# Layer 0 routed experts with 71 tiles in place of 72, and a loop over tiles with a longer written-out end

## The chip, the cores and the metric

One Trainium2 chip, one of its cores. The metric is the device time of one launch of the whole kernel in microseconds (us); all inputs and outputs are in the device's memory. A core has five instruction streams that run side by side and wait for each other by semaphores: PE (TensorE; the profile shows its weight loads apart as PEld), DVE (VectorE), ACT (ScalarE), POOL (GpSimd) and SP (SyncE, here used to issue DMAs). Each stream is a program of its own, with its own loops and branches, and its instructions are brought from memory by DMA too: the profile has them as packets of a kind "instruction", one queue for each engine (q8 is PE's, q14 is DVE's).

## What is computed

A two-layer network on x, 16 batches x 256 tokens x 512 channels (4096 tokens). Cut to what matters:

```python
def reference(x, ctx, g_xattn, g_ffn, ...):
    x = x + tanh(g_xattn[0]) * wkv(w, u, layernorm(x), ctx)              # decaying running average over the tokens
    x = x + tanh(g_ffn[0])   * moe0(layernorm(x))                        # 8 experts, each token uses 2; one shared
    x = x + tanh(g_xattn[1]) * chunked_causal_attention(layernorm(x), ctx, ctx)   # 16 heads of 32, 256 tokens
    x = x + tanh(g_ffn[1])   * moe1(layernorm(x))                        # 64 experts, each token uses 6, room for 64

def moe0(xf):                                                            # 4096 x 512
    ew, ei = top_k(xf @ gate_w.T, 2)
    ew = softmax(ew)
    routed = sum over the 2 chosen e of  ew * ((silu(xf @ w_gate[e].T) * (xf @ w_up[e].T)) @ w_down[e].T)
    return routed + sigmoid(xf @ se_gate_w.T) * shared(xf)
```

The change concerns `routed` of moe0, which the kernel calls its phase `routed0`.

## The kernel before

The kernel runs through four phases, one after the other, with a barrier of all engines between them (L164): `wkv_phase` (layer 0's attention part and the routing and shared expert of moe0, 16 batches), `routed0_phase` (the 8 experts of moe0), `attention_phase` (layer 1's attention, routing and shared expert, 16 batches) and `routed1_phase` (the 64 experts of moe1, in 32 pairs).

**The tiles of routed0.** 4096 tokens choose 2 experts each, which gives 8192 pairs of a token and an expert. They lie in a list in memory, sorted by expert, and each expert's part is worked on in tiles of 128 pairs, the last of an expert with dummies in its open places. 8192 / 128 = 64 tiles would do if each expert's count were a multiple of 128. Each expert may leave one tile part filled, and the kernel runs `TILES0 = N * K0 // P + E0 = 72` of them (L24). An expert's last tile lacks at most 127 pairs, so that (8192 + 8 x 127) / 128 = 71.9 bounds the number of tiles that hold a pair: no routing fills more than 71. The tile past those that the routing fills has all 128 places on a dummy row: it is gathered, run through the matmuls like any other, and its results go to a place out of bounds, which the write leaves out. `tiles_table` works out for each of the 72 tiles its expert and its start in the list, in arrays of 128 x 72 and 128 x 72 x 8.

**One tile.** SP loads the tile's 128 pairs (L2191), POOL gathers the 128 token rows (L2194), PE transposes them (L1047, four blocks; the helper L332 is one matmul of a product of numbers split in a high and a low part), ACT and DVE copy the transposed rows as high part (L1107) and low part (L1161), PE does gate and up (12 matmuls at L332), ACT the silu (L1124), DVE its product with up (L1149), PE transposes h (L1070), ACT and DVE split it (L1112, L1155, L1156), PE does down (L1079 twice as the profile counts, and three at L332), DVE scales by the pair's weight (L1175) and POOL writes the rows out (L1019). The code of one turn of PE holds the transposes of the next tile, gate and up of this one and down of the one before, so that tiles overlap. The turns differ by the tile's place in a ring of `WAYS0 = 8`, since buffers and semaphores are chosen by it (`pair_0` to `pair_7`, `ys_0` to `ys_3`).

**The loop over tiles.** Every engine runs `turns(eng, TILES0, turn, WAYS0)` (L107). It writes out the first `ways + 1` turns, then makes a loop of `count // ways - 2` iterations whose body has `ways` turns, and then writes out the turns that are left. For 72 tiles by eights these are 9 turns (tiles 0 to 8), 7 iterations of 8 (tiles 9 to 64) and 7 turns (tiles 65 to 71). A loop of 7 iterations branches back 6 times. The same helper makes the loops of the two batch phases (16 batches by twos: 3 turns, 6 iterations of 2, 1 turn, so 5 branches back) and of PE in routed1.

**The code behind it.** On each engine the instructions stand in the order of the phases: the loop of `attention_phase` comes after all turns of routed0 that are written out. In the compiled program of DVE an instruction takes 64 bytes. Counted there, the attention loop's first instruction, to which it branches back, is number 1023 of DVE's stream, and its last is number 1373. That is 351 instructions. For PE the loop's first instruction is number 5272, for ACT 667.

Of the kernel before, what the change touches and what calls it, by code (L numbers as in the profile page):

```python
# [14 lines left out]
P = 128  # L15
B, T, C = 16, 256, 512
N = B * T
# [3 lines left out]
DUMMY = P  # L21
E0, H0, S0, K0 = 8, 256, 512, 2
E1, H1, S1, K1, CAP = 64, 352, 704, 6, 64
TILES0 = N * K0 // P + E0  # L24
UNUSED = 2 * K0 * N
LIST0 = E0 * N + P
HEADS, D = 16, 32
# [8 lines left out]
WAYS0, SLOTS0, AHEAD0, READY0 = 8, 4, 3, 2  # L36
# [20 lines left out]
class Chain:  # L57
# [5 lines left out]
    def turn(self, i):  # L63
        assert self.n in (0, self.per), (self.n, self.per)
        self.n, self.base = 0, i * self.per
# [35 lines left out]


def last(count, ways=2):
    return Turn(count - 1, count // ways - 1, ways - 1, count, ways)


def turns(eng, count, turn, ways=2):  # L107


    assert count % ways == 0  # L110
    for n in range(ways + 1):
        turn(Turn(n, n // ways, n % ways, count, ways))
    with eng.Fori(1, count // ways - 1) as j:
        for n in range(1, ways + 1):
            turn(Turn(ways * j + n, j + n // ways, n % ways, count, ways))
    for n in range(count - ways + 1, count):
        turn(Turn(n, n // ways, n % ways, count, ways))


# [13 lines left out]


FIRST, LAST = first(B), last(B)


# [40 lines left out]
class Setup:  # L178
# [35 lines left out]
    def pool(self, nc, pool):  # L214
# [14 lines left out]
                       allow_small_or_imprecise_dtypes=True).then_inc(made, 1)  # L229
        nc.gpsimd.iota(c.tile_no[:], [[1, TILES0]], base=0, channel_multiplier=0,  # L230
                       allow_small_or_imprecise_dtypes=True).then_inc(made, 1)
# [104 lines left out]
def wkv_phase(nc, io, c):  # L336
# [6 lines left out]
    with Memory(nc, "wkv_") as m:  # L343
# [6 lines left out]
        count_i = m.sb("count_i", [P, E0], I32)  # L350
        past = m.sb("past", [P, TILES0, E0])
        past_nt = m.sb("past_nt", [P, TILES0, E0])
        expert, start, row = (m.sb(n, [P, TILES0]) for n in ("expert", "start", "row"))
        table, expert_i, row_i = c.early.table, c.early.expert_i, c.early.row_i
# [55 lines left out]
        with nc.Block() as block:  # L410
# [319 lines left out]
            def _(dve):  # L730
# [119 lines left out]
                def tiles_table():  # L850
# [7 lines left out]

                    every = [P, TILES0, E0]

# [87 lines left out]
def routed0_phase(nc, io, c):  # L948


    with Memory(nc, "routed0_") as m:
# [28 lines left out]
        placed = [m.sem(f"rows_placed{s}") for s in range(SLOTS0)]  # L980
        with nc.Block() as block:
# [5 lines left out]
            def _(sp):  # L987
# [10 lines left out]

                turns(sp, TILES0, turn, WAYS0)

            @block.gpsimd
            def _(pool):
# [33 lines left out]
                turns(pool, TILES0, turn, WAYS0)  # L1036
                place(last(TILES0, WAYS0))
                for s in range(SLOTS0):
                    pool.wait_ge(placed[s], 16 * (TILES0 // SLOTS0))

            @block.tensor
            def _(pe):
# [1293 lines left out]
```

## Time and profile before

| | us |
|---|---|
| three runs | 2252.53, 2248.7, 2243.45 (median 2248.7) |
| the profiled execution, its own time | 2247.8 |
| its span, first to last instruction | 2246.1 |
| routed0's tiles, first silu to the last result's write | 546 to 912 |
| attention, first instruction after the barrier | 917.5 |
| attention's loop on DVE (6 iterations) | 1099.6 to 1743.7 |
| routed1 | 1850 to 2246 |

The span of 2246.1 us lies within 1.7 us of that execution's own time. So a us that is lost or won inside is a us of the time. An engine's share of the span (PE 87%, DVE 58%, POOL 39%, ACT 34%) is a mean over the four phases; the 40 slices of section 2 of the page, 56 us each, show them apart. A row of the timeline is: start, duration, engine, line, operation, output and inputs; in brackets the idle time of the engine ahead of it and what ended it, where "issue" means that no wait in the profile explains it. A row of busy time by stretch is: start and end, length, then for PE, PEld, DVE, ACT and POOL the busy us and in brackets the number of instructions, then the granted TensorE clock (1.00 is 2.4 GHz), the busy share of the DMA engines and the GB/s moved. A row of packets is: queue and kind, packets, MB, the packets' share of 16 engines in that stretch. A row of a line's instructions is: line, engine, operation, count, shortest/median/longest in ns, and the start of the first and the last.

### The profile page before, as it was taken

The numbers are of one execution on the slowest core, as the hardware profiler recorded it, in microseconds if no ns is written. First come the engines' busy times: TensorE is split into PE (matmuls) and PEld (weight loads), VectorE is DVE, ScalarE is ACT, GpSimd is POOL, SyncE is SP. The second block draws the span as 40 slices with busy tenths as digits, with TensorE's granted clock in tenths as the row PEclk, the third lists the DMA queues.
The fourth block names the chain that finished last, engine by engine and source line by source line (L and its number), as shares of the span: only waits on it lengthen the run. The fifth ranks groups of instructions, "written<-read, shape, count | busy, mean of one in ns | idle before, by whom it ended". The sixth has DMA issues, their size and how long they took to land. (4 is left out here: it accounts for less than half of the span.)

```text
span 2246.1 us, 38784 instructions
## 1 busy us (share of the span) xinstructions
PE 1964.9 (87%) x11898; PEld 1394.6 (62%) x11899; DVE 1299.3 (58%) x3013; ACT 757.8 (34%) x2192; POOL 864.8 (39%) x840
## 2 busy tenths in 40 slices
PE   3898888988999999469999999999999969989886
PEld 2666666665777777347777777777777754433332
DVE  6888888885644444237776767776766632222221
ACT  3323333324322222255554545554545411111111
POOL 5556655544543333142333333333333241121221
PEclk9999999999999999669999999999999989989998
DMA  8323222223333332331111121111111249999995
GB/s 257 130 85 94 75 85 83 84 92 101 104 102 102 102 103 95 131 99 67 67 67 68 67 68 67 68 67 68 67 67 67 99 183 416 403 405 404 404 406 173
DMA packets 113560, 319.47 MB, mean 142 GB/s; under 512 B 31298, under 2 KB 39490, under 8 KB 105220
## 3 DMA queue, kind: packets, MB, share of 16 engines
q1 hardware_dynamic: 86388, 264.83, 31.4%
q0 software_dynamic: 26880, 52.68, 8.2%
q8 instruction: 88, 1.44, 0.3%
q14 instruction: 60, 0.49, 0.1%
q10 hardware_dynamic: 144, 0.03, 0.0%
HBM read 257.33 MB, written 62.33 MB: 142 GB/s over the span
## 5 line engine op out<-in xcount | busy, mean ns | idle before, releaser
L1585 ACT ACTIVATE attn_pr<-attn_score_ps,attn_nmax 128x128 f32<-128x128 f32 x496 | 201.5, 418 | 201.2 <-DVE attn_nmax L1733 201.2
L1696 POOL DMA_INDIRECT list<-attn_pair,attn_pos x192 | 191.0, 995 | 65.2 <-issue 61.3
L332 PE MATMUL attn_ffn_ps<-attn_xnT_high,attn_wgu_high 128*128 128x256 f32 x704 | 208.2, 296 | 8.2 <-DVE attn_hT_low L1825 7.3
L332 PE MATMUL attn_ffn_ps<-attn_xnT_low,attn_wgu_high 128*128 128x256 f32 x704 | 199.8, 284 | 0.0
L332 PE MATMUL attn_ffn_ps<-attn_xnT_high,attn_wgu_low 128*128 128x256 f32 x704 | 199.6, 283 | 0.0
L304 POOL TENSOR_SCALAR attn_norm_var_eps<-attn_norm_mean_var 128x2 f32<-128x2 f32 x32 | 7.9, 247 | 474.5 <-DVE attn_norm_mean_var L298 474.5
L532 PE MATMUL wkv_ffn_ps<-wkv_xnT,wkv_wg 128*128 128x256 f32 x512 | 147.3, 439 | 25.1 <-DVE wkv_x L847 24.0
L1981 POOL DMA_INDIRECT out<-routed_ym,routed_place x32 | 50.2, 1568 | 294.7 <-DMA out<-routed_ym,routed_place 274.5
L1733 DVE TENSOR_REDUCE attn_nmax<-attn_score_ps 128x2 f32<-128x256 f32 x248 | 126.3, 551 | 62.9 <-PE attn_score_ps L1422 61.9
L332 PEld LDWEIGHTS attn_ffn_ps<-attn_xnT_high,attn_wgu_high 128*128 128x128 f32 x704 | 135.3, 192 | 18.3 <-DVE attn_hT_low L1825 12.1
L1019 POOL DMA_INDIRECT y<-routed_ys,first_ffn_pair x72 | 73.3, 1017 | 186.1 <-DVE routed_ys L1175 176.3
L532 PEld LDWEIGHTS wkv_ffn_ps<-wkv_xnT,wkv_wg 128*128 128x128 f32 x512 | 107.9, 219 | 50.7 <-DVE wkv_x L847 31.4
L332 PEld LDWEIGHTS attn_ffn_ps<-attn_xnT_low,attn_wgu_high 128*128 128x128 f32 x704 | 135.6, 193 | 0.0
L332 PEld LDWEIGHTS attn_ffn_ps<-attn_xnT_high,attn_wgu_low 128*128 128x128 f32 x704 | 135.3, 192 | 0.0
L1432 PE MATMUL attn_tr_ps<-ident,attn_pr 128*128 128x128 f32 x768 | 115.1, 288 | 21.5 <-ACT attn_pr L1585 21.3
L532 PE MATMUL wkv_ffn_ps<-wkv_xnT,wkv_wu 128*128 128x256 f32 x512 | 122.8, 383 | 0.0
L332 PE MATMUL routed_gu_ps<-routed_wgu_high,routed_xT_high 128*128 x288 | 120.3, 418 | 2.0 <-POOL first_ffn_wgu_low L976 1.8
L1738 DVE COPY second_ffn_room<-attn_tr_ps 128x384 f32<-128x384 f32 x96 | 52.9, 551 | 118.0 <-PE attn_tr_ps L1432 93.3
L1419 PE MATMUL attn_score_ps<-second_ffn_room 32*128 32x256 f32 x992 | 118.7, 358 | 0.7 <-issue 0.7
L332 PE MATMUL routed_gu_ps<-first_ffn_wgu_low,routed_xT_high 128*128 x288 | 113.8, 395 | 0.0
L332 PE MATMUL routed_gu_ps<-routed_wgu_high,routed_xT_low 128*128 x288 | 113.2, 393 | 0.0
L1432 PEld LDWEIGHTS attn_tr_ps<-ident,attn_pr 128*128 128x128 f32 x768 | 87.0, 145 | 41.2 <-issue 32.9
(286 smaller groups left out, 4790.0 us busy)
## 6 DMA issues: line engine op xcount, KB each, us to landing
second_ffn_room<-in_w_gu SPq DMA_DIRECT2D x16, 2816.0 KB, 31.2
routed_wgu<-in_w_gu SPq DMA_DIRECT2D x16, 2816.0 KB, 31.4
second_ffn_room<-in_w_down SPq DMA_DIRECT2D x16, 1536.0 KB, 24.5
routed_wdn<-in_w_down SPq DMA_DIRECT2D x16, 1536.0 KB, 26.1
wkv_x<-in_x SPq DMA_DIRECT2D x32, 512.0 KB, 3.8
second_ffn_room<-y SPq DMA_DIRECT2D x32, 512.0 KB, 5.6
wkv_vT<-in_ctxT SPq DMA_DIRECT2D x16, 512.0 KB, 4.3
xn<-wkv_xn SPq DMA_DIRECT2D x16, 512.0 KB, 2.8
```

Of the source, the lines that this page charges most:

```text
L304: nc.gpsimd.tensor_scalar(self.var[:], self.mv[:, :, 1], EPS, None, ALU.add).then_inc(self.rstd_s, 1)
L332: ins = nc.tensor.matmul(out, a[i], b[j], start=start and n == 0, stop=stop and n == 2)
L532: ins = nc.tensor.matmul(ffn_ps[n % 2][:, col:col + T], w[:, k, n * P:(n + 1) * P], xnT[:, k, :], start=(k == 0), stop=(k == KC - 1))
L1019: nc.gpsimd.indirect_dma_start(io["y0"], bass.IndirectOffsetOnAxis(ap=pair[t.s][:, 1:2].bitcast(U32), axis=0), ys[t.s % SLOTS0][:], None, ...
L1419: nc.tensor.matmul(score_ps[:, a, KEYS[j]], qT[b.s][r:r + D, k, j * P:(j + 1) * P], kT[b.s][r:r + D, k, 0:(j + 1) * P], start=(j == 1), st ...
L1432: ins = nc.tensor.transpose(tr_ps[bank][:, col * P:(col + 1) * P], pr[u % 2][:, z // 3, z % 3, :], c.ident[:])
L1585: nc.scalar.activation(pr[u % 2][:, a, j:2 * j + 1, :].rearrange("p k t -> p (k t)"), score_ps[:, a, KEYS[j]], ACT.Exp, bias=nmax[u % 2][: ...
L1696: nc.gpsimd.indirect_dma_start(io["list1"], bass.IndirectOffsetOnAxis(ap=pos[b.s][:, j, k:k + 1], axis=0), pair[b.s][:, j, k, :], None, bo ...
L1733: v.tensor_reduce(nmax[u % 2][:, :, j], score_ps[:, :, KEYS[j]], AX.X, ALU.max, negate=True).then_inc(max_s, 1)
L1738: v.tensor_copy(prT[u % 4][:, 0].rearrange("p k t -> p (k t)"), tr_ps[0][:, 0:3 * P]).then_inc(tr_ev[0], 1)
L1981: nc.gpsimd.indirect_dma_start(io["out"], bass.IndirectOffsetOnAxis(ap=place[q.s % SLOTS1][:].bitcast(U32), axis=0), ym[q.s % SLOTS1][:], ...
```

## The change

`TILES0` is 71. `turns` no longer asks for a multiple of `ways`: the loop still has `count // ways - 2` iterations, and the written-out end begins after the last of them, wherever that is. For 71 tiles by eights: 9 turns (0 to 8), 6 iterations (9 to 56) and 14 turns (57 to 70), so the loop branches back 5 times. For 16 by twos and 32 by eights the turns are the same ones as before. `last()` gives the place of a last tile that needn't end a round, and POOL's last wait takes the number of writes that each of the four `ys` buffers has had.

```diff
-TILES0 = N * K0 // P + E0
+TILES0 = N * K0 // P + E0 - 1
...
 def last(count, ways=2):
-    return Turn(count - 1, count // ways - 1, ways - 1, count, ways)
+    return Turn(count - 1, (count - 1) // ways, (count - 1) % ways, count, ways)
...
-    assert count % ways == 0
     for n in range(ways + 1):
         turn(Turn(n, n // ways, n % ways, count, ways))
     with eng.Fori(1, count // ways - 1) as j:
         for n in range(1, ways + 1):
             turn(Turn(ways * j + n, j + n // ways, n % ways, count, ways))
-    for n in range(count - ways + 1, count):
+    for n in range((count // ways - 1) * ways + 1, count):
         turn(Turn(n, n // ways, n % ways, count, ways))
...
                 for s in range(SLOTS0):
-                    pool.wait_ge(placed[s], 16 * (TILES0 // SLOTS0))
+                    pool.wait_ge(placed[s], 16 * -(-(TILES0 - s) // SLOTS0))
```

One line goes from the file, so every line number behind `turns` is one less after the change.

On each engine the seven turns that are added to the written-out end push what comes behind. The listing of DVE's instructions around the start of attention's loop, before; the branch and the ISA at the helper's line open the loop, and what follows is its first turn:

```order
L298 BN_AGGR attn_norm_mean_var<-attn_norm_stats 128x2 x2
L113 UNCONDITIONAL_BRANCH
L113 ISA
L1738 COPY second_ffn_room<-attn_tr_ps 128x384
L1730 ISA
L1733 TENSOR_REDUCE attn_nmax<-attn_score_ps 128x2 x2
L1828 ISA
L1829 SCALAR_TENSOR_TENSOR attn_x_1<-attn_ffn_ps,gate_half,attn_x_1 128x512
```

And after:

```order
L297 BN_AGGR attn_norm_mean_var<-attn_norm_stats 128x2 x2
L112 UNCONDITIONAL_BRANCH
L112 ISA
L1737 COPY second_ffn_room<-attn_tr_ps 128x384
L1729 ISA
L1732 TENSOR_REDUCE attn_nmax<-attn_score_ps 128x2 x2
L1827 ISA
L1828 SCALAR_TENSOR_TENSOR attn_x_1<-attn_ffn_ps,gate_half,attn_x_1 128x512
```

The instructions are the same and in the same order. What moved is their place in the stream: the loop's branch is row 676 of DVE's listing before and row 711 after. The listing puts some instructions in one row and leaves waits out. In the compiled program the loop's first instruction goes from number 1023 to 1086, 63 further. Its last goes from 1373 to 1436. On PE the loop's first goes from 5272 to 5741, and on ACT from 667 to 709. The loops of `wkv_phase` and of routed0 itself stay where they are.

The end of routed0 on DVE, before, with the buffers' numbers in the names (`ys_2` is the third of four buffers for results):

```order
L1149 TENSOR_TENSOR routed0_h<-routed0_silu_gate,routed0_gu_ps1 128x256
L1175 TENSOR_SCALAR routed0_ys_2<-routed0_y_ps0,first_ffn_pair_6 128x512
L1155 TENSOR_TENSOR routed0_hT_low<-routed0_ht_ps,routed0_hT_high 128x128
L1156 COPY routed0_hT_whole<-routed0_ht_ps 128x128
L1175 TENSOR_SCALAR routed0_ys_3<-routed0_y_ps1,first_ffn_pair_7 128x512
L981 UNCONDITIONAL_BRANCH
```

And after:

```order
L1148 TENSOR_TENSOR routed0_h<-routed0_silu_gate,routed0_gu_ps0 128x256
L1174 TENSOR_SCALAR routed0_ys_1<-routed0_y_ps1,first_ffn_pair_5 128x512
L1154 TENSOR_TENSOR routed0_hT_low<-routed0_ht_ps,routed0_hT_high 128x128
L1155 COPY routed0_hT_whole<-routed0_ht_ps 128x128
L1174 TENSOR_SCALAR routed0_ys_2<-routed0_y_ps0,first_ffn_pair_6 128x512
L980 UNCONDITIONAL_BRANCH
```

The phase ends with the same instructions, one place earlier in the ring: the last tile is 70 in place of 71, and uses `ys_2` in place of `ys_3`.

## Rows read from the trace of the kernel before

**Rows 1.** The page: the span in 40 slices of 56 us, in tenths.

```profile
PE   3898888988999999469999999999999969989886
DVE  6888888885644444237776767776766632222221
PEclk9999999999999999669999999999999989989998
DMA  8323222223333332331111121111111249999995
```

**Rows 2.** Busy time by stretch (columns as in the section on the profile).

```profile
588.60:869.90 281.30, 280.35 (x1289) 212.70 (x1288) 126.44 (x280) 63.72 (x169) 111.67 (x113) 1.00 0.32 101
869.90:903.90 34.00, 34.00 (x157) 25.92 (x156) 15.12 (x34) 7.42 (x20) 11.43 (x12) 1.00 0.25 81
917.00:1000.00 83.00, 43.27 (x256) 29.96 (x256) 26.45 (x57) 39.43 (x116) 29.78 (x25) 0.58 0.43 144
```

**Rows 3.** Timeline of PE in routed0: the down product of two neighbouring tiles.

```profile
869.65 1.02 PE L1079 MATMUL routed_y_ps<-first_ffn_down,routed_hT_whole 128*128 x2
874.64 1.02 PE L1079 MATMUL routed_y_ps<-first_ffn_down,routed_hT_whole 128*128 x2
```

**Rows 4.** The silu of each tile: duration min/median/max in ns, first and last start.

```profile
L1124 ACT ACTIVATE routed_silu_gate<-routed_gu_ps x72: 383/383/384, 546.1 to 904.3; 128x256 f32<-128x256 f32 x72
```

**Rows 5.** Timeline of PEld: the first transpose after one of routed0's branches back.

```profile
630.16 0.42 PEld L1047 LDWEIGHTS routed_xt_ps<-ident,first_ffn_xg 128*128 128x128 f32 x4 [0.61 <-issue]
```

**Rows 6.** Waits from 590 to 903: us in total, times, longest us.

```profile
POOL y L1019 <- DVE routed_ys L1175: 168.3, 61, 4.0
ACT routed_silu_gate L1124 <- PE routed_gu_ps L332: 138.3, 62, 2.2
DVE routed_ys L1175 <- PE routed_y_ps L332: 46.7, 63, 0.8
```

**Rows 7.** Timeline from the last tile to the first instruction of attention.

```profile
909.10 0.75 DVE L1175 TENSOR_SCALAR routed_ys<-routed_y_ps,first_ffn_pair 128x512 f32<-128x512 f32 x1 [2.10 <-PE routed_y_ps L332]
910.69 0.98 POOL L1019 DMA_INDIRECT y<-routed_ys,first_ffn_pair  x1 [2.27 <-DVE routed_ys L1175]
917.54 0.20 DVE L1871 TENSOR_SCALAR attn_limit<-base 128x64 f32<-128x64 f32 x1 [7.70 <-PEq L164]
```

**Rows 8.** The loop's branch: DVE in attention, DVE in routed0, ACT in attention.

```profile
L113 DVEq COMPARE_BRANCH  x1: 63/63/63, 1313.8 to 1313.8; - x1
L113 DVEq FUSED_REGOPS  x1: 85/85/85, 1318.4 to 1318.4; - x1
L113 DVEq COMPARE_BRANCH  x1: 74/74/74, 630.1 to 630.1; - x1
L113 DVEq FUSED_REGOPS  x1: 70/70/70, 630.3 to 630.3; - x1
L113 ACTq COMPARE_BRANCH  x1: 45/45/45, 1308.0 to 1308.0; - x1
L113 ACTq FUSED_REGOPS  x1: 78/78/78, 1308.2 to 1308.2; - x1
```

**Rows 9.** Timeline of DVE: first instruction behind each of attention's five branches.

```profile
1210.05 0.56 DVE L1738 COPY second_ffn_room<-attn_tr_ps 128x384 f32<-128x384 f32 x1 [5.00 <-issue]
1318.53 0.56 DVE L1738 COPY second_ffn_room<-attn_tr_ps 128x384 f32<-128x384 f32 x1 [4.61 <-issue]
1425.21 0.56 DVE L1738 COPY second_ffn_room<-attn_tr_ps 128x384 f32<-128x384 f32 x1 [4.77 <-issue]
1532.16 0.56 DVE L1738 COPY second_ffn_room<-attn_tr_ps 128x384 f32<-128x384 f32 x1 [5.32 <-issue]
1640.31 0.56 DVE L1738 COPY second_ffn_room<-attn_tr_ps 128x384 f32<-128x384 f32 x1 [4.91 <-issue]
```

**Rows 10.** Timeline: what DVE does behind that branch, and the PE that waits.

```profile
1319.01 1.01 DVE L1733 TENSOR_REDUCE attn_nmax<-attn_score_ps 128x2 f32<-128x256 f32 x2
1319.93 0.74 DVE L1829 SCALAR_TENSOR_TENSOR attn_x<-attn_ffn_ps,gate_half,attn_x 128x512 f32<-128x512 f32 x1
1320.73 0.66 PE L1401 MATMUL attn_ffn_ps<-ident,attn_xn 128*128 128x128 f32 x4 [1.11 <-DVE attn_x L1829]
```

**Rows 11.** Instruction packets by queue: whole kernel, 1250:1357, 1315:1318, 1320:1323.

```profile
q8 instruction: 88, 1.44, 0.3%
q14 instruction: 60, 0.49, 0.1%
q8 instruction: 9, 0.15, 0.5%
q14 instruction: 5, 0.04, 0.1%
q14 instruction: 1, 0.01, 1.4%
q14 instruction: 1, 0.01, 0.7%
```

**Rows 12.** Timeline of PEld behind the loop's branch near 1205.

```profile
1206.88 0.19 PEld L332 LDWEIGHTS attn_ffn_ps<-attn_wd_high,attn_hT_high 128*128 128x128 f32 x1
1208.75 0.19 PEld L332 LDWEIGHTS attn_ffn_ps<-attn_wd_low,attn_hT_high 128*128 128x128 f32 x1 [1.69 <-issue]
```

**Rows 13.** Timeline of PEld: the same transposes in three batches in a row.

```profile
1251.72 0.64 PEld L1432 LDWEIGHTS attn_tr_ps<-ident,attn_pr 128*128 128x128 f32 x6 [1.49 <-issue]
1304.19 0.64 PEld L1432 LDWEIGHTS attn_tr_ps<-ident,attn_pr 128*128 128x128 f32 x6 [1.49 <-issue]
1359.77 0.64 PEld L1432 LDWEIGHTS attn_tr_ps<-ident,attn_pr 128*128 128x128 f32 x6 [1.49 <-issue]
```

## The prediction

> **What bounds the kernel now.** I read the page's 40 slices first, since the phases have different limits, and the change touches one phase and moves the code of the ones behind it [rows 1]. routed0 is slices 10 to 16: PE is at 9 there and DVE at 4. In its steady part PE is busy 280.35 of 281.30 us, and 34.00 of 34.00 in its last stretch, at a clock of 1.00 [rows 2]. The table of waits agrees: ACT, POOL and DVE all wait for what PE or the one behind PE makes, and PE has no row of that size [rows 6]. So routed0 costs what PE's matmuls cost. Attention is slices 19 to 31: PE is at 9 again, but I looked there for the branches of its loop, because that code is moved. Its first 83 us run at a mean clock of 0.58, whatever stands ahead of them in routed0 [rows 2]. routed1 is bound by DMA (9 in its slices) and is left as it is.
>
> **The tile that goes.** Two tiles in a row stand 874.64 - 869.65 = 4.99 us apart [rows 3]. The silu confirms 72 tiles between 546.1 and 904.3, a mean of 5.05 with the slower first ones [rows 4]. PE runs without a gap in the last stretch, so nothing hides the tile: -4.99. The tile that goes is a late one, with no work on the expert's weights. Its gather, list load and write on POOL and SP go too. They lie under PE. The end of the phase, from the last tile's scaling at 909.10 to attention's first instruction at 917.54, has the same steps on one tile earlier [rows 7], and costs what it did. The arrays of the tile table shrink from 72 to 71 columns, which is 1/72 of a few DVE operations, under 0.1 us.
>
> **The branch that goes.** The loop branches back 5 times in place of 6. Behind a branch PE's weight load has a gap of 0.61 us which no wait explains [rows 5]. Against the steady period of 4.99, the six tiles behind a branch come 0.38, 0.40, 0.36, 0.39, 0.33 and 0.12 us late. One of them goes: -0.33, between -0.12 and -0.40. Sum of the direct parts: -5.3.
>
> **The longer written-out end.** 14 turns in place of 7 are read once, in a row. PE has about 67 instructions in a turn, so a packet of 16 KB (below) lasts some four tiles, 19 us, and fetching one took under 5 us wherever I could see it. The written-out end of before shows no stop in PE: busy 34.00 of 34.00 [rows 2]. Cost 0. If that cover were gone, each of two more packets would cost 2 to 5 us. DVE, ACT and POOL have 9, 6 and 8 instructions in a turn, and wait half of the time [rows 6].
>
> **The moved code: where the sum is decided.** Attention's loop branches back 5 times, on every engine. Behind DVE's branch at 1313.8 the next instruction starts at 1318.4. The same branch in DVE's routed0 loop takes 630.1 to 630.3, and ACT's in attention 1308.0 to 1308.2 [rows 8]. All five of DVE's stand 4.61 to 5.32 us with nothing waited for [rows 9]. What fills that time is a fetch of instructions: an iteration has 5 packets of 0.04 MB on q14, 8 KB or 128 instructions each, one of them between branch and resumption, and the next about 3 us after the resumption, in 1320 to 1323 [rows 11]. In 640 to 860, inside routed0's loop, no queue has an instruction packet. The same transposes of PE stand 1304.19 - 1251.72 = 52.47 us apart without a branch and 1359.77 - 1304.19 = 55.58 with one [rows 13]. Over the five branches the surplus is 1.5 to 3.6 us, 12.5 in all: half of DVE's stop comes through to PE.
>
> Why does DVE's loop fetch and ACT's doesn't? DVE's has 351 instructions. ACT's has 262, three blocks of 128. I take it that DVE holds four blocks, one of which is the one being fetched ahead. A loop that touches four has thrown out its first by the time it branches back. Where the blocks begin comes from PE: after a branch back it stops for 1.69 us, at 1208.75, in the middle of a product in which nothing is waited for [rows 12], and again for 1.13 at 1638.51. Counted in the program that is the 42nd instruction of the loop, number 5314. So PE's blocks of 256 (16 KB packets on q8) have 62 instructions ahead of the stream's first. If DVE has the same 62 (the times of its packets in straight code allow 61 to 67), its loop starts at (1023 + 62) mod 128 = 61 of a block before, and 67 instructions of that block follow: enough to run while the next block comes. **After the change it starts at (1086 + 62) mod 128 = 124.** Four instructions are left: set the registers, the copy at L1738, a register, and one of the two reductions at L1733. The block with the rest isn't there. It was usable about 4.9 us after resumption before, since the next packet came 2.9 to 3.3 us behind the resumption and an instruction runs some 1.9 us behind its packet. So the second reduction, which began 0.9 us after the resumption [rows 10], begins 4.9 after it: 4.0 us later. PE already waits 1.11 us for the L1829 that follows it [rows 10], so nothing is left to hide it. I take 3.8 of the 4.0, since PE's own stop of 1.69 goes (its loop start gets 85 instructions of rest in place of 42). Bounds: 3 (part absorbed as with the first stop) to 5 (a whole second stop, as in rows 9); the floor is 0, if the next block is fetched together with the first. Five branches: 5 x 3.8 = +19.0, from +15 to +25.
>
> The loop still touches four blocks (124 + 351 = 475, under 512), so its first stop stays. ACT's loop goes from offset 89 to 3 of a block and touches three both times. POOL's and SP's stay small.
>
> **Sum**, against the profiled execution's own 2247.8 (the median of the runs is 0.9 above it): 2247.8 - 5.0 - 0.3 + 19.0 = **2261.5**, for this case 2256 to 2268.
>
> A rule of the Trainium skill stands against this. Its page "Runtime: NRT & Kernel Launch", section "Instruction fetch mechanics", has an engine's instruction memory refilled in blocks of 16 KiB, prefetched in order, says that a taken branch whose target isn't in the window forces a fetch before execution goes on, and therefore favours unrolling. The trace agrees on the fetch behind a taken branch, but DVE's packets are 8 KB here. With 256-instruction blocks the loop would have a long rest either way, and the sum would be rival A's.
>
> **Rivals.**
> A: *the place of the code doesn't matter.* Either the next block is asked for together with the first, or my 62 is wrong by enough to leave a long rest. Then only the direct parts count: 2247.8 - 5.3 = **2242.5**. For it: I have not seen DVE stop for want of a second block, and the 62 is carried over from PE. Against it: PE did stop so, in two of five branches, when its second packet came 4.4 us behind the first. 0.19.
> B: *the loop's start falls on or just behind a block's start.* That takes 66 or 67 ahead in place of 62. Then the loop touches three blocks, as ACT's does, it stays in the buffer, and DVE's five stops go with the 12.5 us that they cost: 2247.8 - 5.3 - 12.5 = **2230**. For it: four instructions decide, and packet times allow it. Against it: PE's stop gives 62 exactly. 0.11.
> C: *a second stop at each branch*, the forecast and the case on the slower side. It decides if between 1 and 6 instructions of rest are left behind the branch, and is slower as soon as a stop costs over 5.3 / 5 = 1.1 us: **2261.5**. 0.70.
> That the change doesn't do what it says is no case of its own: the tile is in the program whatever its rows hold (72 silus [rows 4]), so dropping it drops its work. Attention's slow clock at its start hangs on PE's idle time at the barrier, which stays.
>
> **How the numbers follow.** The predicted time is C's. The range reaches from A's 2242.5, less 1.5 for the branch's and the runs' spread, to C's upper end: 2241 to 2268. It leaves out B and the ends of C. The three runs lie within 0.25% of their median, so that 0.5% (11.2 us) is about what can be told from no change. B is faster by more. A is within. C is slower by over 0.5% where its sum is above 2259.5, about two thirds of its chance: slower 0.47, and same 0.19 + 0.23 = 0.42.
>
> **What would show each step.** The window of routed0's tiles shorter by 5.3 us, silu x71, PE gapless up to the last tile. DVE's first instruction behind each of attention's five branches still 4.6 to 5.3 us late, and then a second gap with "issue" as its reason ahead of the second L1732 or the first L1828, 3 to 5 us: C. No such gap, the first ones as they were: A. None of both and fewer q14 packets in an iteration: B. The period of the transposes with a branch would be 58 to 60 us in C, about 55 in A and 52.5 in B. PE's stop of 1.69 should be gone in all. The forecast is wrong if DVE's blocks aren't where I counted them, or if the fetch of the second block starts before the first is used.

## The result, and the profile after

The change makes the kernel slower. In the median the kernel before takes 2251.8 us (8 runs) and the changed one 2269.5 us (8 runs, 2263.9 to 2279.7). The ratio is 1.008 with a 95% interval of 1.0061 to 1.0099. The prediction said slower, by +13.7 us, and gave 2241 to 2268. The direction and the place were right. The size was too small, and the median lies 1.5 us above the range.

The profiled execution took 2268.25 us with a span of 2266.5, against 2246.1 before. It divides at three instructions that both traces have: the last silu of a tile, and DVE's first and sixth branch at the end of attention's loop.

| stretch | before | after | difference |
|---|---|---|---|
| start to the first silu | 546.1 | 544.1 | -2.0 |
| first to last silu (72 or 71 tiles) | 358.2 | 353.0 | -5.2 |
| last silu to DVE's first branch | 300.7 | 303.1 | +2.4 |
| five iterations, first branch to sixth | 538.7 | 562.2 | **+23.5** |
| sixth branch to the end | 502.4 | 504.1 | +1.7 |
| sum | 2246.1 | 2266.5 | +20.4 |

The tiles, from the silu's row of after, whose columns are those of [rows 4]:

```profile
L1123 ACT ACTIVATE routed_silu_gate<-routed_gu_ps x71: 383/383/384, 544.1 to 897.1; 128x256 f32<-128x256 f32 x71
```

The branch of attention's loop on DVE, of after (count, shortest/median/longest in ns, first and last start):

```profile
L112 DVEq COMPARE_BRANCH  x6: 55/63/63, 1200.2 to 1762.4; - x6
```

And of before:

```profile
L113 DVEq COMPARE_BRANCH  x6: 55/63/63, 1205.0 to 1743.7; - x6
```

The tiles gave 5.2 us, as the sum had it. The first, third and last stretch vary by themselves: over all kernels below, the first silu stands between 544.1 and 551.8, and the third stretch is 299.6 to 303.4 long (b72_others apart, of which more below). a71_dve2 and a71_dve4, two instructions apart, stand at 299.6 and 303.2. The kernels with 72 tiles have 300.4 to 301.9 and those with 71, but for a71_dve2, 302.1 to 303.4, so that some of the +2.4 may belong to the change; no run separates it. What stands out is the loop.

DVE behind its branches back, timeline of after. [rows 9] have one stop for each branch, here are two:

```profile
1205.61 0.56 DVE L1737 COPY second_ffn_room<-attn_tr_ps 128x384 f32<-128x384 f32 x1 [5.30 <-issue]
1210.35 1.02 DVE L1732 TENSOR_REDUCE attn_nmax<-attn_score_ps 128x2 f32<-128x256 f32 x2 [4.18 <-issue]
...
1317.95 0.56 DVE L1737 COPY second_ffn_room<-attn_tr_ps 128x384 f32<-128x384 f32 x1 [5.57 <-issue]
1322.83 1.02 DVE L1732 TENSOR_REDUCE attn_nmax<-attn_score_ps 128x2 f32<-128x256 f32 x2 [4.32 <-issue]
...
1435.13 1.02 DVE L1732 TENSOR_REDUCE attn_nmax<-attn_score_ps 128x2 f32<-128x256 f32 x2 [4.85 <-issue]
```

The second stop is there at all five branches, 4.18, 4.32, 4.85, 4.25 and 4.30 us. It stands ahead of *both* reductions, so that fewer instructions ran between the stops than the four that the prediction counted. The register instruction ahead of the reductions tells how many. It comes at the end of the second stop, in a row of that line:

```profile
L1729 DVEq FUSED_REGOPS  x1: 46/46/46, 1210.3 to 1210.3; - x1
```

Only the first register instruction and the copy ran before. With two instructions of rest, 64 instructions lie ahead of DVE's stream, not 62.

Who waits for it is PE, on PE's timeline of after. At the same branch [rows 10] have a wait of 1.11 us, and in PE's own timeline of before eight of these matmuls take 1.31:

```profile
1212.09 1.97 PE L1400 MATMUL attn_ffn_ps<-ident,attn_xn 128*128 128x128 f32 x8 [5.04 <-DVE attn_x L1828]
...
1324.57 1.97 PE L1400 MATMUL attn_ffn_ps<-ident,attn_xn 128*128 128x128 f32 x8 [5.93 <-DVE attn_x L1828]
```

PE waits 5.0 to 5.9 us at each branch, and then its eight matmuls take 1.97 us in place of 1.31. That is its clock, which had fallen to half before PE went on. Busy time by stretch over the 16 us behind a resumption, of after:

```profile
1317.95:1333.95 16.00, 10.07 (x71) 7.92 (x74) 5.77 (x10) 5.35 (x20) 10.54 (x8) 0.79 0.34 124
```

And of before:

```profile
1318.53:1334.53 16.00, 14.88 (x126) 11.73 (x126) 8.82 (x19) 8.15 (x32) 10.80 (x9) 1.00 0.42 150
```

The mean granted clock there is 0.79 behind four of the five branches of after (0.89 behind the first). In before it is 1.00 behind four (0.89 behind the one of [rows 9] with the longest stop). From the start of the eight matmuls to the first product of the shared expert behind them (L331, L332 in before) PE needs 6.28 us at the second branch, where before needs 5.02, with the same instructions between. So the half clock costs 1.26 us there. Over the five branches it is 1.1 in the mean, since one of before's runs at half too (6.37 us).

What the loop as a whole pays is read from PE's busy time in it. Busy time by stretch, the five iterations of before and of after:

```profile
1205.00:1743.70 538.70, 502.75 (x4093) 402.87 (x4092) 374.67 (x941) 270.00 (x950) 195.27 (x220) 0.99 0.20 70
1200.20:1762.40 562.20, 505.59 (x4095) 407.95 (x4096) 374.62 (x941) 270.92 (x950) 195.19 (x220) 0.97 0.19 67
```

PE does the same work in both. It is idle for 36.0 us before and 56.6 after, which is 20.6 of the 23.5. The other 2.8 are busy time, the same matmuls at a lower clock: 30.7 us of the loop are granted at half in place of 10.2, and 18.0 of the 30.7 fall on PE's work (the rest on its wait).

### The profile page after: what moved, and what is told of

Its sections match the earlier page's. It is cut to its first block and busy times, and to the rows that moved or that the text cites. A ratio compares the mean times of both kernels' runs of the same rounds, so it can differ in the third digit from the quotient of the medians.

```text
span 2266.5 us, 38608 instructions
## 1 busy us (share of the span) xinstructions
PE 1959.9 (86%) x11875; PEld 1395.0 (62%) x11876; DVE 1297.1 (57%) x3008; ACT 757.6 (33%) x2189; POOL 862.4 (38%) x838
## 5 line engine op out<-in xcount | busy, mean ns | idle before, releaser
L331 PE MATMUL attn_ffn_ps<-attn_xnT_high,attn_wgu_high 128*128 128x256 f32 x704 | 208.4, 296 | 5.1 <-DVE attn_hT_low L1824 3.4
L331 PE MATMUL attn_ffn_ps<-attn_xnT_low,attn_wgu_high 128*128 128x256 f32 x704 | 199.8, 284 | 0.0
L331 PE MATMUL attn_ffn_ps<-attn_xnT_high,attn_wgu_low 128*128 128x256 f32 x704 | 199.6, 283 | 0.0
L331 PEld LDWEIGHTS attn_ffn_ps<-attn_xnT_high,attn_wgu_high 128*128 128x128 f32 x704 | 135.4, 192 | 15.3 <-DVE attn_hT_low L1824 9.0
L531 PEld LDWEIGHTS wkv_ffn_ps<-wkv_xnT,wkv_wg 128*128 128x128 f32 x512 | 107.8, 219 | 50.7 <-DVE wkv_x L846 31.5
L331 PEld LDWEIGHTS attn_ffn_ps<-attn_xnT_low,attn_wgu_high 128*128 128x128 f32 x704 | 135.7, 193 | 0.0
L331 PEld LDWEIGHTS attn_ffn_ps<-attn_xnT_high,attn_wgu_low 128*128 128x128 f32 x704 | 135.3, 192 | 0.0
L331 PE MATMUL routed_gu_ps<-routed_wgu_high,routed_xT_high 128*128 x284 | 118.6, 417 | 2.0 <-POOL first_ffn_wgu_low L975 1.5
L549 PE MATMUL wkv_ffn_ps<-wkv_wd,wkv_hT 128*128 128x512 f32 x256 | 112.5, 592 | 0.0
L331 PE MATMUL routed_gu_ps<-first_ffn_wgu_low,routed_xT_high 128*128 x284 | 112.3, 395 | 0.0
```

The costliest lines, as they stand in the source:

```text
L331: ins = nc.tensor.matmul(out, a[i], b[j], start=start and n == 0, stop=stop and n == 2)
L531: ins = nc.tensor.matmul(ffn_ps[n % 2][:, col:col + T], w[:, k, n * P:(n + 1) * P], xnT[:, k, :], start=(k == 0), stop=(k == KC - 1))
L549: ins = nc.tensor.matmul(ffn_ps[j][:], hT[:, k, j * P:(j + 1) * P], wd[:, k, :], start=(k == 0), stop=(k == M0 - 1))
```

## The experiments

All of them add waits on a semaphore that has been satisfied for long, at the end of routed0, where each engine stands idle for several us. They do no work; they move the code behind them. The edit for DVE, here with 65:

```diff
                 scaled(last(TILES0, WAYS0))
+                for _ in range(65):
+                    dve.wait_ge(y_s, 1)
+                    alone(dve)
```

`alone` keeps the waits from being joined, so each is one instruction. In every compiled program the number of the loop's first instruction was counted again. In a name, a71 or b72 is the kernel that it starts from, and the rest is how many waits are added on which engine. The theory is that of the prediction, mended in one number: DVE holds its code in four blocks of 128, one of them the one fetched ahead, with 64 instructions ahead of the stream. A loop that touches four blocks is fetched anew at each branch back, and if its first instruction stands n before a block's end, with n small, there is a second stop n instructions later.

| kernel | loop starts at | place in block, blocks touched | five iterations, us | PE in them: idle, busy, clock at half | ratio to before, 95% |
|---|---|---|---|---|---|
| before | 1023 | 63, 4 | 538.7 | 36.0, 502.8, 10.2 | 1 |
| after | 1086 | 126, 4 | 562.2 | 56.6, 505.6, 30.7 | 1.008 (1.0061 to 1.0099) |
| a71_dve65 | 1151 | 63, 4 | 539.2 | 35.9, 503.3, 10.2 | 0.9993 (0.9978 to 1.0008) |
| b72_dve63 | 1086 | 126, 4 | 562.1 | 54.9, 507.2, 37.5 | 1.0089 (1.0067 to 1.011) |
| b72_others | 1023 | 63, 4 | 544.8 | 37.1, 507.7, 20.5 | 1.0178 (1.0151 to 1.0206) |
| a71_dve2 | 1088 | 0, 3 | 529.4 | 30.0, 499.4, 3.4 | 0.9922 (0.9897 to 0.9948) |
| b72_dve65 | 1088 | 0, 3 | 532.7 | 30.4, 502.3, 10.2 | 0.9958 (0.9939 to 0.9977) |
| a71_dve30 | 1116 | 28, 3 | 530.0 | 30.6, 499.4, 3.4 | 0.9942 (0.9922 to 0.9961) |
| a71_dve40 | 1126 | 38, 4 | 534.9 | 33.4, 501.5, 6.8 | 0.9976 (0.9955 to 0.9996) |
| a71_dve2_pe88 | 1088 | 0, 3 | 527.9 | 27.6, 500.3, 6.8 | 0.9942 (0.9919 to 0.9965) |
| b72_dve61 | 1084 | 124, 4 | 568.0 | 53.8, 514.2, 47.8 | 1.0099 (1.0072 to 1.0126) |
| b72_dve55 | 1078 | 118, 4 | 540.1 | 36.6, 503.5, 10.2 | 1.0001 (0.9986 to 1.0017) |
| a71_dve4 | 1090 | 2, 3 | 528.2 | 30.3, 497.8, 0 | 0.9911 (0.9889 to 0.9933) |

"Five iterations" is each trace's sixth branch less its first, as in the two rows above. PE's column is in us of the same stretch, the last number what the clock was granted at 1.2 GHz, half of its full 2.4. Both are of one trace for each kernel; the ratio is of 4 to 10 runs of the kernel and 8 to 28 of before. One by one, from branch to branch, in us:

| kernel | iterations |
|---|---|
| before | 108.8, 106.5, 106.5, 108.5, 108.4 |
| after | 112.1, 112.5, 112.5, 112.5, 112.6 |
| a71_dve65 | 106.8, 107.0, 106.9, 106.8, 111.7 |
| a71_dve40 | 107.8, 106.3, 106.2, 108.4, 106.1 |
| a71_dve30 | 105.9, 106.6, 105.8, 105.9, 105.8 |
| b72_others | 109.0, 106.9, 108.3, 109.1, 111.5 |

### 71 tiles with DVE's loop back in its place

> The changed kernel (71 tiles) with 65 waits on a semaphore that is long satisfied, added on DVE at the end of routed0, where DVE stands idle for 7.7 us before attention. With them attention's loop on DVE starts at instruction 1151 in place of 1086, which in blocks of 128 is the same place as before's 1023. Theory 1 (the loop's place in DVE's blocks makes the second stop): one stop of about 5 us behind each of DVE's five branches as in before, no second one; time = before less 5.3 us, ratio 0.998, some 23 to 25 us under the changed kernel. Theory 2 (the longer written-out end, or the moved code of PE, ACT or POOL costs the time, and DVE's second stop comes along): it stays slow, ratio 1.008 as the changed kernel.

The time is 2249.9 us, the ratio 0.9993, and the loop 539.2 us. All 71 tiles, the long written-out end and the moved code of PE, ACT and POOL are in it, and the slowdown is gone. DVE's timeline has one stop again behind each branch (4.91 to 5.12 us). Theory 2 falls with it. The ratio is a little above the 0.998 expected. 0.9 us of that is at the barrier: DVE's first instruction of attention stands 14.1 us behind the last silu in place of 13.2. The time of the waits isn't what does it. DVE has run all 65 of them 4.4 us before that instruction, and b72_dve65 with as many has 13.3. The three kernels with 71 tiles and 30, 40 or 65 waits on DVE have 14.1 to 14.3, each with an instruction packet of q14 in that time, but a71_dve2_pe88 has 14.0 without one. The cause stays open.

### 72 tiles with DVE's loop where the change puts it

> The kernel before (72 tiles, 7 turns at the end) with 63 such waits on DVE at the end of routed0: attention's loop on DVE starts at instruction 1086, exactly where the change puts it, and nothing else is touched. Theory 1: DVE shows the second stop of 4.2 to 4.9 us ahead of its first reduction behind each branch back, PE's wait there goes from 1.1 to 1.8 us to 5.0 to 5.9, and the time is before + 25 us, ratio 1.011. Theory 2: nothing but 63 short instructions in idle time is added, ratio 1.000.

The other way around: 63 instructions that do nothing, and the kernel takes 2272.0 us, 1.0089. The loop takes 562.1 us against 562.2 of the changed kernel. Timeline of DVE:

```profile
1323.34 0.56 DVE L1741 COPY second_ffn_room<-attn_tr_ps 128x384 f32<-128x384 f32 x1 [5.57 <-issue]
1328.15 1.02 DVE L1736 TENSOR_REDUCE attn_nmax<-attn_score_ps 128x2 f32<-128x256 f32 x2 [4.25 <-issue]
```

And of PE:

```profile
1329.88 1.97 PE L1404 MATMUL attn_ffn_ps<-ident,attn_xn 128*128 128x128 f32 x8 [6.36 <-DVE attn_x L1832]
```

The same two stops, a wait of PE of 5.2 to 6.4 us at the five branches, the same half clock. The two runs together show that the loop's place on DVE is the cause of the longer loop, and all of it: undone, 539.2 us are left, and alone it gives 562.1.

### The other engines' code moved, DVE's not

> The kernel before with such waits on the other engines and none on DVE: 469 on PE, 42 on ACT, 56 on POOL at the end of routed0, so that attention's loops on PE, ACT and POOL stand where the change puts them, and DVE's where it was. Theory 1: no second stop on DVE; PE's own stops of 1.7 and 1.1 us inside the shared expert's products are gone; the 469 waits of PE take some us at the barrier, of which part may show; ratio 0.999 to 1.005, and attention's loop as long as before (644 us). Theory 2: the loop is longer by some 25 us, ratio 1.01.

The total, 1.0178, is far off what I expected. What it shows is the price of the tool. DVE's timeline at the start of attention; [rows 7] have 7.70 us there:

```profile
958.45 0.20 DVE L1880 TENSOR_SCALAR attn_limit<-base 128x64 f32<-128x64 f32 x1 [49.96 <-PEq L164]
```

PE's 469 waits hold the barrier for 42.3 us longer (ACT's 42 and POOL's 56 run beside them), 0.09 us each at least, since PE's idle time there hides some of them. The median is 41.8 us above that of before's runs beside it. So this kernel speaks only by its loop: DVE has one stop at each branch, as Theory 1 has it, but the five iterations take 544.8 us in place of 538.7. Two of its five stops are long, 5.48 and 5.75 us. Behind the fifth, of 4.86 us, PE's clock is 0.79 in the mean over 16 us, and that iteration takes 111.5 us. In the whole loop PE is idle for 1.1 us more than before and busy for 4.9 more, with 20.5 us at the half clock in place of 10.2. So the 6 us are mostly clock. a71_dve65, with PE's, ACT's and POOL's loops in the same places, has 539.2 us, so they don't belong to the move.

### 71 tiles with DVE's loop at the start of a block

> The changed kernel with 2 such waits on DVE at the end of routed0: attention's loop on DVE starts at instruction 1088, two further. If 64 instructions lie ahead of the stream's first (in the changed kernel's trace only two instructions run between the two stops), that is the first of a block, and the 352 instructions of the loop lie in three blocks. Theory 1 with its second part (four blocks are held, one of them the one fetched ahead): no stop at all behind DVE's five branches, no packets on q14 inside the loop but at its ends; time = before - 5.3 - 12.5 = 2234, ratio 0.992. Theory 1 without it (every branch back of this length fetches): one stop of 5 us as before, no second one, ratio 0.998. Theory 2: ratio 1.008.

Two instructions more than the changed kernel, and it takes 2232.8 us: 0.9922, rival B's case. DVE's branch and the next instruction, rows of the branch's line:

```profile
L112 DVEq COMPARE_BRANCH  x1: 56/56/56, 1304.6 to 1304.6; - x1
L112 DVEq FUSED_REGOPS  x1: 85/85/85, 1304.9 to 1304.9; - x1
```

0.3 us as in routed0's loop [rows 8], in place of 4.6. The packets of 1150 to 1700, of this kernel:

```profile
q8 instruction: 46, 0.75, 0.6%
q14 instruction: 2, 0.02, 0.0%
```

And of before:

```profile
q8 instruction: 45, 0.74, 0.5%
q14 instruction: 27, 0.22, 0.1%
```

DVE's loop, of 351 instructions as the program has them (352 in the expectation, which changes no block), stays in its buffer once it touches three blocks. PE's idle time in the loop falls from 36.0 us to 30.0.

### 72 tiles at the start of a block

> The kernel before (72 tiles) with 65 satisfied waits on DVE at the end of routed0, so that attention's loop on DVE starts at instruction 1088, the first of a block. It tells apart what 71 tiles are worth by themselves. Theory 1: no stop behind DVE's branches, loop some 12.5 us shorter than before's; against the 71-tile kernel with the same place it is 5.3 us longer: ratio 0.995. If the gain of the 71-tile kernel with its loop at 1088 came from anything else that the change moved, this one stays at 1.000.

0.9958 and a loop of 532.7 us: most of the gain is the place, with or without the 72nd tile. Against a71_dve4 and a71_dve2 this kernel is 0.36 to 0.47 percent longer, which is 8 to 11 us, and the tile with its branch is 5.2 of that. 3.3 to 4.5 us of the rest are in the loop. They are not idle time of PE, which is 30.4 us here, 30.0 in a71_dve2 and 30.3 in a71_dve4. They are busy time, 502.3 against 499.4 and 497.8, with 10.2 us of the loop at the half clock in place of 3.4 and 0. So it is clock, and why it falls more often in this kernel the runs don't show.

PE's own stop is there in all three, in another place. With PE's loop where it was, it stands inside the shared expert's products, on PE's timeline of b72_dve65:

```profile
1316.18 0.39 PE L332 MATMUL attn_ffn_ps<-attn_wd_high,attn_hT_high 128*128 128x512 f32 x1 [1.21 <-issue]
```

It is long at two of five branches (1.21 and 1.19 us). No kernel that starts from 71 tiles has such a row. They have one at the branch itself instead, here from after:

```profile
1200.66 0.87 PE L1431 MATMUL attn_tr_ps<-ident,attn_pr 128*128 128x128 f32 x6 [0.92 <-issue]
```

All stops behind the five branches that no wait explains, in the rows of PE's matmuls, add up to 2.7 us in before and in b72_dve65, to 2.9 in after, and to 2.8 and 3.1 in a71_dve2 and a71_dve4. The prediction's rest of 85 instructions in place of 42 moved PE's stop. It didn't take it away.

### The edge between three blocks and four

> The changed kernel with 30 satisfied waits on DVE: the loop starts at 1116, place 28 of its block by 64 ahead, and its 352 instructions end at place 379 of 384, so that it still lies in three blocks. Theory 1 (it is the number of blocks touched): no stop, ratio 0.992 to 0.993. If it takes a start on the first place of a block: one stop of 5 us at each branch, ratio 0.998.

> The changed kernel with 40 satisfied waits on DVE: the loop starts at 1126, place 38 of its block, and ends at place 389, in a fourth block. Only ten waits more than the run with 30. Theory 1: the first stop of about 5 us is back at all five branches, no second one (90 instructions of rest), ratio 0.997 to 0.999, 12 us above the run with 30. If the buffer holds more than the theory says, no stop and 0.993.

30 waits: no stop, no packet of q14 but 2 in the same 550 us, 530.0 us. 40 waits: 26 packets and all five stops, DVE's timeline of that kernel:

```profile
1314.35 0.56 DVE L1740 COPY second_ffn_room<-attn_tr_ps 128x384 f32<-128x384 f32 x1 [5.00 <-issue]
1420.67 0.56 DVE L1740 COPY second_ffn_room<-attn_tr_ps 128x384 f32<-128x384 f32 x1 [5.02 <-issue]
```

Ten instructions of place bring five stops of 5 us back. What they cost is less than the 12 us I gave: 4.9 us in the loop, 0.0034 in the ratio. a71_dve65 less a71_dve2 is the same comparison at other places and gives 9.8 us, b72_dve65 against before 6.0. In PE's idle time the three comparisons are 2.8, 5.9 and 5.6 us. So DVE's first stop, hidden in large part, goes with 1 to 2 us a branch in the mean and not 2.5, and 0.6 to 1.2 of that are PE's waiting. The rest of the 4.9 and the 9.8 is busy time, 2.1 and 3.9 us. The long single iterations show it: 107.8 in a71_dve40 (its first, with 3.4 us at the half clock 100 us behind the branch) and 111.7 in a71_dve65, where PE had waited 1.44 us and its clock then fell to 0.79 in the mean over 16 us.

### PE's loop in seven blocks

> The 71-tile kernel with DVE's loop at the first place of a block (2 waits) and PE's loop moved to place 3 of its block of 256 by 88 satisfied waits on PE at the end of routed0, which its idle time at the barrier should hide (469 took 39 us, so 88 take 7). The 1727 instructions of PE's loop then lie in 7 blocks in place of 8. If PE holds 8 blocks, one being fetched, the way DVE holds 4, then PE's instruction packets inside the loop (9 in 107 us) go. The branch costs PE little already with DVE's stop gone: an iteration takes 105.9 us against twice 52.5. So the time is 0 to 4 us under the 71-tile kernel with 2 waits: ratio 0.990 to 0.993. If 88 waits show at the barrier it is up to 2 us over it.

PE's packets in 1150 to 1700 go from 46 to 3, rows of this kernel:

```profile
q8 instruction: 3, 0.05, 0.0%
q14 instruction: 2, 0.02, 0.0%
```

PE keeps its code in the same way, by blocks of 256, with a loop of 1727 instructions in seven of them. PE's own stops behind the branches are gone too, 2.8 us in a71_dve2 and none here, and its idle time falls from 30.0 us to 27.6. The loop is 1.5 us shorter (527.9 against 529.4), which is about what a71_dve2 and a71_dve4 differ by. The ratio, 0.9942, is not told apart from a71_dve2's. The barrier comes 0.9 us later than in a71_dve2, but so it does in a71_dve30, without a wait on PE.

### How much rest: four instructions, and ten

> The kernel before with 61 satisfied waits on DVE: attention's loop starts at 1084, two earlier than the change puts it, so that by 64 instructions ahead of the stream four run between the two stops: registers, the copy, a register, one reduction. That is the case that the prediction's sum worked out. The second stop then stands ahead of the second reduction, 3.9 to 4.0 us long. If the stop's length alone sets the price (5 x 3.8, the prediction's sum), time = before + 19, ratio 1.0085, attention's five iterations 19 us longer than before's 538.7 (557.7). If PE's clock drops after its wait of 5 us whatever stands behind it and adds 1.2 us to each branch, they are about 561, ratio 1.0095.

This is the case that the prediction worked out, and the second stop is what it said: 3.79 to 3.95 us, ahead of the second reduction. DVE's timeline:

```profile
1329.26 0.56 DVE L1741 COPY second_ffn_room<-attn_tr_ps 128x384 f32<-128x384 f32 x1 [6.26 <-issue]
1333.96 0.69 DVE L1736 TENSOR_REDUCE attn_nmax<-attn_score_ps 128x2 f32<-128x512 f32 x1 [3.82 <-issue]
```

But the loop takes 568.0 us, 29.3 more than before's and not 19. Both numbers that I expected were too low. Busy time by stretch of this kernel:

```profile
1329.26:1345.26 16.00, 10.86 (x51) 7.34 (x51) 5.76 (x10) 5.46 (x20) 10.57 (x8) 0.68 0.27 98
```

The mean clock over the 16 us is 0.68 behind three branches and 0.79 behind two. The same query over the whole loop of this kernel, as above for before and after, tells the two parts of the price:

```profile
1209.00:1777.00 568.00, 514.15 (x4093) 411.46 (x4092) 374.31 (x941) 271.15 (x950) 195.12 (x220) 0.96 0.19 66
```

PE is idle for 53.8 us, 17.8 more than in before. That is the 19 of the sum, or a little less. The other 11.4 of the 29.3 are busy time. 47.8 us of the loop are at the half clock, and behind the three worst branches 8.0 to 9.2 us of that fall on PE's work, where after has 3.1 to 4.0. A shorter stop than after's with more work at the half clock costs more. Why the clock stays down longer here I can't say from these runs.

> The kernel before with 55 satisfied waits on DVE: the loop starts at 1078 and ten instructions run before the block ends, among them both additions at L1829 for which PE waits. The second stop then stands ahead of L1836, which waits for ACT anyway: in before it runs 3.9 us after the resumption, here 4.8. Theory 1 (the price depends on what stands behind the block's end and on who waits for it): a stop is seen on DVE but PE's wait for L1829 stays at 1 to 2 us with its clock at 1.00 behind it, at most 1 us a branch: five iterations 539 to 544 us, ratio 1.000 to 1.002. If any second fetch costs the same: 562 us, ratio 1.01.

Ten instructions of rest, and the second fetch costs nothing that can be measured: 1.0001, five iterations 540.1 us. DVE's timeline:

```profile
1319.20 1.40 DVE L1832 SCALAR_TENSOR_TENSOR attn_x<-attn_ffn_ps,gate_half,attn_x 128x512 f32<-128x512 f32 x2
1322.58 1.29 DVE L1839 TENSOR_TENSOR attn_xnT_low<-attn_ffn_ps,attn_xnT_high 128x512 fp32r<-128x512 f32 x2 [1.98 <-ACT attn_xnT_high L1625]
```

And PE's, at the same branch:

```profile
1320.00 1.64 PE L1404 MATMUL attn_ffn_ps<-ident,attn_xn 128*128 128x128 f32 x8 [1.32 <-DVE attn_x L1832]
```

The two additions that PE waits for run before the block ends, the next block is late only for an instruction that would wait for ACT, and PE's wait and mostly its clock are before's. PE then waits for that instruction, 0.64 to 0.68 us at four of the five branches, and is idle for 36.6 us in the loop against 36.0. Six instructions between this kernel and the one above make 28 us.

### A version with a margin

> 71 tiles with 4 satisfied waits on DVE: loop at 1090, place 2 of a block, a version with a margin of two instructions against the edge. As the one with 2 waits: no stop behind DVE's branches, five iterations 529 to 530 us, ratio 0.992 to 0.994 with a narrower interval.

2232.3 us against 2250.4, ratio 0.9911 (0.9889 to 0.9933), loop 528.2 us. It beats both kernels: 71 tiles, and four instructions ahead of attention that put DVE's loop into three blocks.

## Why the prediction came out as it did

**The tile and the branch.** -5.3 forecast, -5.2 measured between the first and the last silu, in one trace of each. Right, and the longer written-out end costs nothing there.

**The place of DVE's loop.** The mechanism, the five places and the first stop that stays were forecast as measured, and b72_dve63 and a71_dve65 show it by adding and undoing it alone.

**The number of instructions ahead of the stream.** 62, carried over from PE, was wrong for DVE: it is 64. Two instructions ran between the stops, not four. It moved the second stop from 4.0 to 4.4 us. Rival B hung on the same number. It was two instructions away from the case that happened, not four, and a71_dve2 is that rival.

**The price of the second stop is the step that failed.** The sum took 5 x 3.8 = 19.0. The loop grew by 23.5, 4.7 a branch, and that is why the median rose by 17.7 us where 13.7 were forecast. The working took the stop's length as the price, less a little. As a price in idle time it was nearly right: PE's idle time in the loop grew by 20.6. Its wait for L1829 (L1828 after) grew from 0.26, 1.11, 0.78, 1.77 and 0.19 us to 5.04, 5.93, 5.66, 5.58 and 5.61, by 4.7 in the mean, and other waits shrank by 0.6 a branch, mainly the one for L1825 (4.1 us in the loop before, 1.3 after). What the sum left out is the clock. The wait leaves PE at the half clock behind each branch. That costs 1.1 us a branch there and 2.8 us in the loop, less than five times 1.1 because before loses some to the half clock too, at other places. The sum had no term for it, though [rows 2] showed, with 0.58 at attention's start, what the clock is behind an idle PE. b72_dve61 confirms which term it was: with the very stop that was forecast, 3.8 to 3.95 us, idle time grew by 17.8 us and busy time by 11.4, together 29.3.

The working also took PE's own stop as gone, and 0.2 us a branch off for it. It only moved, 2.7 us in five branches before and 2.9 after.

**The range.** Its upper end was the sum with 5 us a branch, set against one execution of 2247.8, while the median of eight runs of before was 2251.8. Set against that median, the forecast's +13.7 gives 2265.5 and the upper end 2272, and 2269.5 would have lain inside. So the median's being outside is half a matter of where the sum was set. The term that was too small, by 4.5 us, is there either way.

**Rival A** fell: the place of the code does matter. **The -12.5 of rival B** was right as a sum, -5.3 - 12.5 = -17.8 against 0.9922, which is -17.6. It was not all DVE's. b72_dve65 takes DVE's stops away alone and shortens the loop by 6.0 us, a quarter of the 24.6 that the five stops last and not half, as the prediction read. In a71_dve2 it is 9.3, and most of the 3.3 more is PE's busy time, its clock (2.9). Its tiles give 5.2 more. 3 us of the 17.6 are in neither, and within what the third stretch and the first silu vary from trace to trace.

**The rule that stood against the sum.** The Trainium skill's page "Runtime: NRT & Kernel Launch", section "Instruction fetch mechanics", is borne out in that a taken branch to code no longer held costs a fetch, here 4.6 to 6.3 us. Its preference for unrolling is borne out at routed0's branch by some 0.2 us (the 5.2 less a tile's 4.99), against 23.5 us that the longer code cost in a loop behind it. Its block of 256 instructions is what PE's packets show. On DVE the packets are 8 KB, the edge between a71_dve30 and a71_dve40 lies where blocks of 128 put it, and the measurement decides: the second stop came, where blocks of 256 would have left a long rest.

## What to carry to other kernels

Writing out more turns of a loop moves every loop behind it, on every engine, against the blocks in which code is fetched. Count where a hot loop starts and ends: in DVE's case three blocks of 128 were free, four cost a stop of 5 us at each branch, and a first instruction 2 or 4 ahead of a block's end cost a second. A handful of instructions ahead of the loop is enough to choose, and a stop on an engine that TensorE waits for should be priced with the clock that TensorE loses behind it: 2.8 us on top of 20.6 in after, and 11.4 on top of 17.8 in b72_dve61.

## What the runs showed that I had not expected

- After a wait of 5 to 6 us inside a busy phase, PE's clock is at half: 0.79 in the mean over the 16 us behind DVE's resumption, 0.89 once in after, and 0.68 three times in b72_dve61. Behind waits up to 2.2 us it was mostly at 1.00, but 0.79 behind one of 1.44 us in a71_dve65 and one of 1.30 in b72_others. What tells these from the others I don't know.
- A satisfied wait on PE takes 0.09 to 0.11 us, so it is no free filler there: 469 of them put the barrier off by 42.3 us, and PE's last matmul ends 50.8 us ahead of attention's first instruction.
- PE holds 1727 instructions in seven blocks without fetching, and fetches eight or nine packets in an iteration when the same loop touches eight blocks.
- A second fetch stop can be free. With ten instructions ahead of the block's end the loop is 1.4 us longer than before's, with four 29.3.
- How often PE's clock is at half in the loop differs from kernel to kernel by more than the edits explain, from 0 us (a71_dve4) to 10.2 (before, a71_dve65, b72_dve65, b72_dve55), and it moves the loop by some us. A difference of that size between two traces should be split into idle and busy time before it is given a cause.
